# A four-layer network on one core: attention's outputs stay turned and are scaled after packing, three programs are joined, and expert 0's places and lists come first

## What is computed

```python
# attention: 16 heads of 16, 4 key heads
q = _rope((x @ Wqa @ Wqb).reshape(b, s, 16, 16)); kv = (x @ Wkva @ Wkvb).reshape(b, s, 4, 16, 2)
k, v = _rope(kv[..., 0]), kv[..., 1]          # each repeated for 4 heads
scores = einsum('bqhd,bkhd->bhqk', q, k) * 16 ** -0.5, causal
out = einsum('bhqk,bkhd->bqhd', softmax(scores), v).reshape(b, s, 256) @ Wout + bout
# experts that choose their tokens
probs = softmax(einsum('BTC,CE->BTE', x, gate_w))
top_p, top_idx = top_k(probs transposed to (B, E, T), 256)
xin = x at top_idx;  y = gelu(xin @ w1) @ w2 * top_p;  out = zeros, y added at top_idx
```

## Time and profile before

| | us |
|---|---|
| median of 3 runs (2562.51 to 2564.99) | 2563.05 |
| the profiled execution | 2565.26 |
| its span | 2563.5 |
| attention's block, from its first matmul to its last VectorE operation | 1456.95 to 1952.63 |
| output projection and norm | 1953.76 to 2012.8 |
| search, places, lists, first gather | 2012.8 to 2086.4 |
| experts, to the end | 2086.4 to 2563.5 |

### The profile page before, as it was taken

How to read it: one execution, slowest core, us unless ns; L and a number is a source line. 1 busy time by engine, 2 the same in 40 slices (tenths; PEclk the granted TensorE clock), 3 DMA queues, 4 the chain that set the end, 5 groups by cost and what they waited for, 6 DMA issues and landing times. The chain is left out here.

```text
span 2563.5 us, 35108 instructions
## 1 busy us (share of the span) xinstructions
PE 2265.3 (88%) x11484; PEld 1336.4 (52%) x11485; DVE 1779.8 (69%) x2586; ACT 1340.3 (52%) x2581; POOL 1346.8 (53%) x1026
## 2 busy tenths in 40 slices
PE   8995889989989987699977699999998559999998
PEld 3442444544544544699964344444445326666666
DVE  6998999999999997655557788888883741111100
ACT  4777887788788785322225456666665211111110
POOL 1545999899899894377756222222222123333432
PEclk9997999999999999799987799999999769999999
DMA  5357345125124113644446522222200503333322
GB/s 164 146 188 259 105 133 186 46 79 172 50 92 155 50 50 103 175 73 70 72 87 142 130 34 33 36 44 36 34 3 4 198 25 67 82 70 68 74 51 25
DMA packets 149681, 231.17 MB, mean 90 GB/s; under 512 B 26257, under 2 KB 98897, under 8 KB 149394
## 3 DMA queue, kind: packets, MB, share of 16 engines
q1 hardware_dynamic: 120258, 190.25, 24.7%
q0 software_dynamic: 29280, 39.11, 9.5%
HBM read 152.23 MB, written 81.66 MB: 91 GB/s over the span
## 5 line engine op out<-in xcount | busy, mean ns | idle before, releaser
L1263 POOL TENSOR_TENSOR scan_hC<-scan_h,scan_c_all 128x1024 f32<-128x1024 f32 x256 | 613.0, 2420 | 65.1 <-DVE scan_h L1118 63.8
L1118 DVE TENSOR_TENSOR_SCAN scan_h<-scan_dA,banks 128x1024 f32<-128x1024 f32 x224 | 504.6, 2276 | 21.6 <-ACT scan_dA L1040 12.9
L893 PE MATMUL banks<-scan_hC,all_ident 128*128 128x512 f32 x1024 | 487.5, 600 | 26.4 <-DVE scan_xc L1125 26.4
L2346 ACT ACTIVATE attn_pt<-banks 128x1024 f32<-128x1024 f32 (+3 forms) x384 | 292.3, 810 | 186.3 <-PE banks L2293 184.8
L1033 ACT ACTIVATE scan_scaled<-mamba_duT,mamba_bT 128x128 f32<-128x128 f32 x1024 | 312.0, 388 | 22.7 <-PE banks L870 22.3
L2230 POOL TENSOR_SCALAR_AFFINE_SELECT attn_pt<-attn_pt 128x256 f32<-128x256 f32 x256 | 104.2, 413 | 382.4 <-ACT attn_pt L2346 380.8
L2364 DVE TENSOR_REDUCE attn_m_lo<-banks 128x1 f32<-128x512 f32 (+3 forms) x432 | 266.8, 662 | 30.1 <-PE banks L2249 19.9
L893 PEld LDWEIGHTS banks<-scan_hC,all_ident 128*128 128x128 f32 x1024 | 185.3, 191 | 179.3 <-issue 129.2
L3068 DVE TENSOR_TENSOR ffn_y<-banks,ffn_gates 128x512 f32<-128x512 f32 x32 | 22.1, 692 | 334.2 <-PE banks L2828 327.5
L3124 POOL DMA_INDIRECT out<-ffn_y,ffn_ids x64 | 105.3, 1646 | 270.4 <-DVE ffn_y L3068 260.6
L2249 PE MATMUL banks<-attn_K,attn_Q 96*128 96x512 bf16 (+3 forms) x768 | 232.1, 340 | 11.1 <-DVE attn_mask L2358 10.0
(11 more groups left out here) (353 smaller groups left out, 3851.2 us busy)
## 6 DMA issues: line engine op xcount, KB each, us to landing
scan_c_all<-scratch_bc SPq DMA_DIRECT2D x64, 512.0 KB, 6.2
ffn_w<-in_e_w SPq DMA_DIRECT2D x16, 1024.0 KB, 5.4
attn_Q<-scratch_q SPq DMA_DIRECT2D x96, 128.0 KB, 4.1
scratch_x<-front_xc SPq DMA_DIRECT2D x8, 1024.0 KB, 5.8
scratch_z<-front_zs SPq DMA_DIRECT2D x8, 1024.0 KB, 7.5
scan_xc<-scratch_x SPq DMA_DIRECT2D x16, 512.0 KB, 3.7
scan_zs<-scratch_z SPq DMA_DIRECT2D x16, 512.0 KB, 4.7
scratch_dt<-front_lw SPq DMA_DIRECT2D x7, 1024.0 KB, 4.1
```

The source lines that it names most:

```text
L893: mm = pe.matmul(PS[:, YB + i, :], ident[:, :], hC[:, u % NHC, i * BANK:(i + 1) * BANK], start=s == 0, stop=s == NST - 1, skip_group_check ...
L1118: dve.tensor_tensor_scan(h[:, u % NH, :], decay, drive, 0.0, ALU.mult, ALU.add).then_inc(scanned, 1)
L1263: pool.tensor_tensor(hC[:, u % NHC, :], h[:, u % NH, :], c_all[:, s, :], ALU.mult).then_inc(hC_done, 1)
L2346: act.activation(pt[:, at % 4, 2 * pair:2 * pair + 2, 0:width], PS[:, ST + 2 * pair:ST + 2 * pair + 2, 0:width], ACT.Exp, scale=HD ** -0.5 ...
```

## The change

Attention's outputs aren't turned any more. ScalarE copies the turned halves to `ot` as before; SP writes a unit's `ot` to DRAM (`send`) and, a unit later, reads the 16 value rows of each head back at their place in `dense`, channels by tokens, and the sum's row of each head spread over 16 partitions into `sums` (`take`, eight transfers). VectorE takes the reciprocal of 64 rows of `sums` (`invert`) and GpSimd multiplies (`scale`), both for unit w - 2 behind step 4 of unit w; those of the last two units stand in the projection. `turn_out`, `divide_out`, `turn_o` and `copy_oT` go, and the projection reads `dense`. The wait for q's and k's stores moves into attention, behind the first round of maxima; the last three calls share one clearing. In the last layer the ranks, places and values of expert 0 are made first, then its lists, then those of the other seven; all values are VectorE's; the compare of a digit is cut into 6 and 2 tiles.

```diff
-SHARES = (3, 3, 5, 2, 3, 5, 4, 4, 5, 3, 3, 2)
+SHARES = (3, 3, 4, 2, 3, 4, 4, 4, 5, 3, 3, 2)
...
+class HeadOutputs:
+    def __init__(self, nc, n):
+        self.dense, self.ot, self.sums = right("o_dense", [P, KC, TOK]), right("ot", [P, SEQ]), right("sums", [P, SEQ])
+        self.dram = scratch(nc, "o", [NU, P, SEQ])
+    def send(self, sp, w):
+        sp.wait_ge(self.copied, 2 * w + 2)
+        sp.dma_start(self.dram[w, :, :], self.ot[:, :]).then_inc(self.put, 16)
+    def take(self, sp, w):
+        b, kv = divmod(w, NKV)
+        sp.wait_ge(self.put, 16 * (w + 1))
+        if w >= 2:
+            sp.wait_ge(self.scaled, w - 1)
+        for j in range(GH):
+            first = kv % 2 * GH * HD + j * HD
+            to = slice(first, first + HD)
+            sp.dma_start(self.dense[to, kv // 2, b * SEQ:(b + 1) * SEQ], self.dram[w, j * VW:j * VW + HD, :]
+                         ).then_inc(self.taken[w % 2], 16)
+            sp.dma_start(self.sums[to, :], self.dram[w, j * VW + HD:j * VW + HD + 1, :].to_broadcast([HD, SEQ])
+                         ).then_inc(self.taken[w % 2], 16)
+    def invert(self, dve, w):
+        rows = slice(w % 2 * GH * HD, (w % 2 + 1) * GH * HD)
+        dve.wait_ge(self.taken[w % 2], 16 * 2 * GH * (w // 2 + 1))
+        dve.reciprocal(self.sums[rows, :], self.sums[rows, :]).then_inc(self.inverted, 1)
+    def scale(self, pool, w):
+        own = self.dense[rows, kv // 2, b * SEQ:(b + 1) * SEQ]
+        pool.wait_ge(self.inverted, w + 1)
+        pool.tensor_tensor(own, own, self.sums[rows, :], ALU.mult).then_inc(self.scaled, 1)
...
@@ attention, SP
             send_maxima(0, 0)
+            for out in out_sem:
+                sp.wait_ge(out, 8 * 3 * NCH)
...
                 send_maxima(w, 1)
+                if w:
+                    outs.send(sp, w - 1)
...
                     send_maxima(w + 1, 0)
+                if w:
+                    outs.take(sp, w - 1)
@@ GpSimd, inside the steps
+                    if x == HK and w >= 2:
+                        pool.wait_ge(future_cut, cuts_through(w, x))
+                        outs.scale(pool, w - 2)
@@ ScalarE, copy_out
-                    act.wait_ge(o_step, 2 * w + h - 1)
+                    act.wait_ge(outs.put, 16 * w)
@@ VectorE
+                    if x == HK and w >= 2:
+                        outs.invert(dve, w - 2)
@@ project_scores
             def project(t):
-                pe.wait_ge(oT_copied, t + 1)
+                if t % TPB == 0:
+                    pe.wait_ge(outs.scaled, NKV * (t // TPB + 1))
...
+                if t in (8, 12):
+                    outs.invert(dve, NU - 2 + (t == 12))
@@ choose_experts
-        HI = TPB // 2
+        HI = 6
+        TURNS = (slice(0, 1), slice(1, NE))
...
+            places(0)
             first_lists(0)
             first_lists(1)
+            places(1)
             lists(1, False)
```

More of the change, by code:

```diff
@@ L2119, in unit_events @@
         mine = events[at:at + share]
-        out.append([[e for e in mine[share * i // SLOTS:share * (i + 1) // SLOTS] if e] for i in range(SLOTS)])
+        out.append([mine[share * i // SLOTS:share * (i + 1) // SLOTS] for i in range(SLOTS)])
         at += share
@@ L2486, in project @@
                 for c in range(KC):
[L2487 removed]
+                    mm = pe.matmul(PS[:, OB + t % 2, 0:DM], outs.dense[:, c, t * P:(t + 1) * P], w_out[:, c, :], start=c == 0, stop=c == KC - 1)
                 mm.then_inc(o_psum, 1)
@@ L2776, in _, with ranks @@
                 mm.then_inc(counted, 1)
-            pe.wait_ge(d, MEMBERS_READY)
-            both = member_b[:, :, :, :].rearrange("p a t e -> p (a t e)")
-            pe.matmul(PS[:, 1, :], before_b[:, :], both, start=True, stop=True)
-            pe.matmul(PS[:, 2, :], ones_b[:, :], both, start=True, stop=True).then_inc(ranked, 1)
+            def ranks(q):
+                pe.wait_ge(cast, q + 1)
+                both = member_b[q][:, :, :, :].rearrange("p a t e -> p (a t e)")
+                wide = 2 * NT * width_of[q]
+                pe.matmul(PS[:, EARLIER[q], 0:wide], before_b[:, :], both, start=True, stop=True)
+                pe.matmul(PS[:, WHOLE[q], 0:wide], ones_b[:, :], both, start=True, stop=True).then_inc(ranked, 1)
+            ranks(0)
             def lists(e, b, first):
                 pe.wait_ge(onehot_made, BATCH * e + b + 1)
+                if b == 0 and first:
+                    pe.wait_ge(vals_made, 4 * HALF)
                 if b == 0 and not first:
@@ L2945, in _ @@
                 dve.wait_ge(leveled, 6 * k + 2)
-                for half in range(2):
-                    at = slice(half * HI, (half + 1) * HI)
+                for at in PIECES_OF_TRIAL:
+                    cut = [P, TRIALS, BATCH, at.stop - at.start, NE]
                     dve.tensor_tensor(above[:, :, :, at, :], by_batch[:, None, :, at, :].to_broadcast(cut),
@@ L3240, in attention_layer @@
         heads = (Q, K, q_in)
+        out_sem = [na.sem(f"out_parts{i}") for i in range(2)]
         for_attention = attention_weights(na, g)
```

239 lines of the change are left out of this document (97 added, 142 removed).

## The result

The changed kernel takes **2643.54 us**, the median of 4 runs (2643.28 to 2643.69), against 2563.67 (2562.51 to 2564.99, 4 runs): a ratio of 1.0311 [1.0293, 1.0329], slower by 3.1%. The prediction was 2645. The profiled run took 2643.69 us, with a span of 2642.0 us, 78.5 more than before.

What follows compares the result with a forecast made beforehand. TensorE was taken to bound attention, VectorE close behind. Terms summing to +81.6, mostly attention's +91, took the profiled 2565.26 us to 2646.9; the median, 2.2 lower, gave 2645 us, range 2603 to 2680.

Steps and rivals of the forecast that it cites:

- The division: VectorE's reciprocal over 1024 columns, absent from the trace: 6.55 us, extrapolated from 8, 16 and 32 columns.
- The standstill: Attention, units 2 to 14: TensorE, with three banks for maxima, stands still 5.5 us behind each division.
- The clock: Attention, after each standstill: about 5 us of work at 1.2 GHz instead of 2.4, worth 2.5 us a unit.
- The unit, and attention: Attention: a unit lasts 36.7 us instead of 29.69, 7.0 more; thirteen of them +91 us.
- the turns: Attention: the output turns taken from TensorE save 1.0 us a unit.
- The projection: Projection and second norm: removed turns and waits save, two divisions (+12.5) and the low clock (+4.3) cost; in sum +5.5.
- Places and lists: First membership to first one-hot: 5.3 us instead of 12.8; with 0.5 from GpSimd, -8 us.
- The cover of the other experts' part: Last layer: the other seven experts' part hides under the gathers, fitting by 1 to 2 us.
- The queue: Rival: SP's nine more issues hold ScalarE's copy or the maxima by 1 to 2 us a unit; about 2665; chance 0.05.
- the clock did not hold: Denies the rival that the clock holds after standstills, without 13 x 2.5 and 4.3; 2608 us; chance 0.2.
- dearer: Rival: the long division takes 8.8 us instead of 6.55, 15 times 2.3 us more; 2679 us; chance 0.1.
- cheap: Rival: the long division takes 1.2 us, hides under step 5 and attention gains; 2528 us; chance 0.05.

Runs made afterwards that it cites:

- second experiment: Changed kernel with 22 useless matmuls of 512 columns on TensorE in units 2 to 14, where it stood still: 2613.76 us.
- compact kernel: Changed kernel with the sums divided as 128 partitions of 32 columns before being spread from DRAM, multiplication one unit later: 2528.31 us.
- the fifth: Changed kernel with attention's outputs as before (turned on TensorE, divided by VectorE in 16 columns), the rest of the change kept: 2551.89 us.
- quarters' kernel: Changed kernel with each division in four of 256 columns, behind separate steps or tiles, and the multiplication one unit later: 2598.70 us.

## Why the prediction was right

**The division.** 6.541 us against 6.55. With the experiments' widths the line reads: 32 columns 0.344, 64 columns 0.542, 256 columns 1.738, 1024 columns 6.541; from 256 to 1024 that is 4.803 / 768 = 6.254 ns a column. The rows 5 alone had given 6.25, from widths thirty times smaller. The page "VectorE: DVE Perf Modes" of the Trainium skill, where it explains the eight slices, gives the reciprocal a repeat count of 8; my reading of it, eight times the pace of one operation, would have made 8.8 us, an estimate from that page. The measurement decides against that reading.

**The standstill.** Forecast 5.5 us, measured 5.38 in the unit shown (5.21 in the row's own bracket) and 5.08 in those where the bracket says 4.91, as at 1845.18: the number of banks and the work of step 5 gave it to 0.1 to 0.4 us.

**The clock.** Forecast 2.5 us a unit, by experiment 2.1. The mechanism was right, and so was the length of the low stretch, about 5 us forecast and 5.0 on average. That this agrees so well is in part luck: the forecast had one stretch to go by the earlier trace rows, and single units have 3.3 to 6.4 us. The size was a little high because less than half of the low stretch is lost (second experiment). In the projection the two standstills are 5.85 and 5.87 us, with two low stretches behind them:

```profile
2052.62 5.80 PE L2498 MATMUL banks<-attn_w_out,attn_o_dense 128*128 128x256 f32 x16 [5.85 <-DVE all_X L2593]
2064.29 8.51 PE L2498 MATMUL banks<-attn_w_out,attn_o_dense 128*128 128x256 f32 x24 [5.87 <-DVE all_X L2593]
```

and the clock in the first of them:

```profile
2052.00:2056.00 4.00, 3.38 (x8) 2.75 (x9) 2.32 (x7) 0.00 (x0) 2.34 (x1) 0.50 0.00 0
```

**The unit, and attention.** 36.28 us on average against 36.7: the thirteen units came to 13 x 6.59 = +86 instead of +91, more than the miss of the whole sum (81.6 against 78.5), so other terms cancelled part of it. That is 13 x 0.4 for the clock and 13 x 0.1 for the standstill, less 13 x 0.1 for the turns: without the division a unit is 28.80 us, 0.89 less than 29.69, where I had taken 1.0. The median came nearer still, 2643.54 against 2645, by chance: the forecast put it 2.2 us under the profiled run, and it was 0.15 under it.

**The projection.** From attention's last matmul to the search's first count +5.0, forecast +3.3 with its shares of the ending and the clearings. The compact kernel shows the two sides that nearly cancel, each counted from attention's last copy of outputs. To the first matmul of expert 0's lists it takes 104.4 us (1931.1 to 2035.56), the changed kernel 120.6 (2031.3 to 2151.85), the fifth, with the old outputs, 115.2 (1944.3 to 2059.52): the two divisions cost 16.1 (forecast 12.5 + 4.3 = 16.8), and the turns and copies that are gone bring 10.8 (forecast 7.0 + 1.1 + 3.2, and 1.4 for the ending, 12.7). So it is this gain that was put too high, by 1.9 us.

**Places and lists.** From the first membership to the first one-hot:

```profile
2145.02 0.45 DVE L2986 TENSOR_TENSOR choose_member<-choose_probs,choose_level 128x32 f32<-128x32 f32 x2
...
2150.27 2.56 DVE L3030 TENSOR_TENSOR ffn_onehot<-ffn_lanes,moe_lane 128x1024 bf16<-128x1024 f32 x2
...
2169.30 3.49 DVE L3030 TENSOR_TENSOR ffn_onehot<-ffn_lanes,moe_lane 128x1024 bf16<-128x1024 f32 x3
...
2171.09 0.36 PE L2802 MATMUL banks<-moe_vals,ffn_onehot 128*128 128x10 bf16 x8
```

5.25 us, forecast 5.3, where it was 12.8. The cover of the other experts' part also held, but narrowly. The first of the three one-hots from 2169.30 is done near 2170.5 by their mean, or can be used near 2170.9 if it takes until then as long as the first one-hot of all did (2150.27 to TensorE's start on it at 2151.85). TensorE asks for it at 2171.09, 20.8 us after the first one-hot, so the margin is 0.2 to 0.6 us, where I had put 1 to 2. From the first one-hot to the first hidden tile 1.4 us are gained instead of 0.5. The gathers begin 0.5 us earlier after the first one-hot than before (3.97 against 4.48 us), as forecast; the other 0.9 us was not forecast. It lies in one gather instruction, which took longer in the kernel before:

```profile
2079.61 1.87 POOL L3113 DMA_INDIRECT ffn_xg<-scratch_xn_rows,ffn_ids  x1 [0.30 <-issue]
...
2157.86 1.04 POOL L3120 DMA_INDIRECT ffn_xg<-scratch_xn_rows,ffn_ids  x1 [0.30 <-issue]
```

Why it took longer there stays open. The end grew by 0.6, as counted for the one large clearing (GpSimd's last scatter starts 8.6 us before the end in before, 9.2 in after).

**The rivals.** The queue was not late (fourth experiment), the clock did not hold, the division was neither dearer nor cheap. The cheap one's working, 2528, was met by the two experiments that made it short, 2527.81 and 2528.31: the same sum was right on both sides of the point where it decides. To 1 us that is luck again: the rest brought 12.5 instead of 11.6, the gain of the turns in the projection was 1.9 less.

## What to carry to other kernels

Count a division by its columns, and do it where the numbers are fewest: 4096 sums cost 0.34 us as 128 x 32 and 6.54 us as 64 x 1024 copies of themselves, and spreading them afterwards through DRAM cost nothing that a unit shows. Look at two things on the engine that gets a long instruction: its work in a unit, here 31.7 us against the bound engine's 28.8, and the length of the instruction against what the banks let the bound engine do meanwhile, here 8.3 against 2.8 us. The first gives 2.9 us a unit and the second 5.4, and it was the second that was paid. Behind a long standstill of TensorE add the clock: here 2.1 us for each 5.4. The division in pieces avoided that part in attention.

## What was not expected of the hardware

TensorE was made faster by more work: 286 matmuls whose results nobody reads took the kernel from 2643.5 to 2613.8 us, because the granted clock stayed at 1.00. In the quarters' kernel the clock stayed at 1.00 in attention with TensorE busy 313 of 350 us and idle up to 2.1 us at a time, and fell in the projection with waits of 3.16 and 4.26 us; in the changed kernel, busy 299 of 350, one wait of 4.9 to 5.2 us in a unit brought it to 0.50 for 3.3 to 6.4 us of the work behind it. Why the low stretch differs so from unit to unit behind nearly the same wait, these runs don't tell.
